# A gated two-layer attention kernel: weighted sums once per head group, fp32 transposes of rounded rows, and VectorE's other work at other steps

## The reference

```python
x = x + tanh(g_xattn[0]) * L0_xattn(layernorm(x), ctx)      # 16 heads of 16; keys: 120 of ctx, then 256 of x
x = x + tanh(g_ffn[0])   * L0_ffn(layernorm(x))             # input rounded by one scale for all of x; ternary weights
x = x + tanh(g_xattn[1]) * L1_xattn(layernorm(x), ctx, lens)# rmsnorm, 256x256 product, plus a decaying recurrence over ctx
x = x + tanh(g_ffn[1])   * L1_ffn(layernorm(x))             # each row rounded by its own scale, int8 product
# L0_ffn:  q = clip(round(x / i_scale), -128, 127);  q @ q_weight.T * w_scale * i_scale + bias
# L1_ffn:  q = clip(round(row / row_scale), -127, 127);  (q @ q_rhs) * row_scale * rhs_scale
```

## Time and profile before

| | us |
|---|---|
| median of 3 runs (lowest, highest) | 1207.3 (1205.55, 1210.32) |
| time of the profiled execution | 1205.75 |
| its span, first to last instruction | 1204.0 |
| TensorE busy | 1098.1 |
| VectorE busy | 930.2 |
| ScalarE busy | 869.0 |
| GpSimd busy | 698.9 |

### The profile page before, as it was taken

How to read it: one execution, slowest core, us unless ns; L and a number is a source line. 1 busy time by engine, 2 the same in 40 slices (tenths; PEclk the granted TensorE clock), 3 DMA queues, 4 the chain that set the end, 5 groups by cost and what they waited for, 6 DMA issues and landing times.

```text
span 1204.0 us, 33614 instructions
## 1 busy us (share of the span) xinstructions
PE 1098.1 (91%) x8458; PEld 667.5 (55%) x8458; DVE 930.2 (77%) x2360; ACT 869.0 (72%) x1794; POOL 698.9 (58%) x1259
## 2 busy tenths in 40 slices
PE   3599999999999999999999999999999948878784
PEld 3355555555555555555555555555555426666663
DVE  3877777777777777777777777777777647999997
ACT  2167777777777777777777777777776658999984
POOL 5355555666555555555555666665554136777766
PEclk9599999999999999999999999999999978999997
DMA  4233334343433333333333333333333101222222
GB/s 131 73 93 96 97 99 103 101 101 103 105 102 102 101 102 98 108 101 95 95 95 95 98 102 102 100 103 99 98 91 87 38 21 42 77 84 80 79 86 80
DMA packets 158681, 110.19 MB, mean 92 GB/s; under 512 B 17154, under 2 KB 154788, under 8 KB 158628
## 3 DMA queue, kind: packets, MB, share of 16 engines
q1 hardware_dynamic: 156900, 108.78, 33.3%
q10 hardware_dynamic: 1728, 0.79, 0.2%
HBM read 30.30 MB, written 16.29 MB: 39 GB/s over the span
## 4 chain that ended last, share of the span: by engine, by line
PE 64%; DVE 15%; issue 9%; POOL 3%; DMA 2%; SPq 2%; ACT 2%; DVEq 1%; POOLq 0%; ACTq 0%
PE pv_ps L621 14%; PE ms_ps L606 13%; PE st_ps L596 12%; PE misc L644 9%; PE misc L652 5%; PE misc L647 4%; DVE neg L789 2%; PE aux L668 2%; DVE am L1170 2%; DMA q<-parts 2%; DVE xs L1159 2%; DVE probs L1203 1%; PE aux L673 1%; SPq L398 1%; PE aux L662 1%
## 5 line engine op out<-in xcount | busy, mean ns | idle before, releaser
L789 DVE TENSOR_REDUCE neg<-ms_ps 128x1 f32<-128x376 f32 x1024 | 531.9, 544 | 206.7 <-PE ms_ps L606 200.7
L883 ACT ACTIVATE probs<-st_ps 128x512 f32<-128x512 f32 x768 | 451.3, 599 | 173.7 <-PE st_ps L596 98.3
L606 PE MATMUL ms_ps<-k,q 96*128 96x376 bf16 x1024 | 336.0, 329 | 13.5 <-DVE neg L789 5.4
L596 PE MATMUL st_ps<-q,k 99*128 99x256 bf16 x1536 | 295.5, 274 | 0.1
L621 PE MATMUL pv_ps<-probs,v 128*32 128x256 f32 (+1 forms) x3072 | 245.4, 391 | 0.6 <-ACT oT L899 0.4
L596 PEld LDWEIGHTS st_ps<-q,k 99*128 99x128 bf16 x1536 | 134.5, 98 | 91.8 <-ACT probs L883 28.3
L606 PEld LDWEIGHTS ms_ps<-k,q 96*128 96x128 bf16 x1024 | 98.7, 96 | 144.7 <-DVE neg L789 79.0
L644 PE MATMUL misc<-xnT,wqkvT 128*128 128x256 f32 x512 | 156.8, 391 | 1.5 <-ACT xnT L904 1.5
L511 POOL TENSOR_TENSOR xs<-xs,bias_p 128x256 f32 (+1 forms) x64 | 45.2, 726 | 142.8 <-ACT xn L941 142.8
L621 PEld LDWEIGHTS pv_ps<-probs,v 128*32 128x32 f32 (+1 forms) x3072 | 60.5, 108 | 117.7 <-issue 93.1
L541 POOL TENSOR_TENSOR parts<-qk,parts 128x632 bf16<-128x632 f32 x64 | 88.7, 1386 | 13.2 <-POOL parts L539 13.2
(11 more groups left out here) (187 smaller groups left out, 1775.3 us busy)
## 6 DMA issues: line engine op xcount, KB each, us to landing
k<-parts SPq DMA_DIRECT2D x384, 94.0 KB, 2.8
q<-parts SPq DMA_DIRECT2D x384, 64.0 KB, 2.5
xs<-in_x SPq DMA_DIRECT2D x32, 256.0 KB, 2.8
out_dram<-xn SPq DMA_DIRECT2D x32, 256.0 KB, 2.2
cx<-in_ctx SPq DMA_DIRECT2D x32, 240.0 KB, 3.4
recurrence_input<-u_in SPq DMA_DIRECT2D x32, 120.0 KB, 2.3
plug<-plugs SPq DMA_DIRECT2D x32, 120.0 KB, 3.4
powers<-gath SPq DMA_DIRECT2D x32, 120.0 KB, 3.2
```

The source lines that it names most:

```text
L596: mm = pe.matmul(st_ps[u % SR][:, j * S:(j + 1) * S], k6[0:KM, r, h, k * P:(k + 1) * P], q6[0:KM, r, h, :], start=True, stop=True)
L606: pe.matmul(ms_ps[t][:, 0:KEYS], q6[0:KR, r, h % HU, t * P:(t + 1) * P], k6[0:KR, r, h % HU, 0:KEYS], start=True, stop=True).then_inc(s_ms, 1)
L789: dve.tensor_reduce(neg[:, m, t, h % HU:h % HU + 1], ms_ps[t][:, 0:KEYS], AX.X, ALU.max, negate=True).then_inc(s_red, 1)
L883: act.activation(probs[:, u % PR, :], st_ps[u % SR][:, :], ACT.Exp).then_inc(s_exp, 1)
```

## The change

The ring `probs` grows from 8 to 12 slots. The three weighted sums of a group of heads are issued one behind the other, at steps 1, 7, 13 and 19, in place of one at each odd step; the third of each group stands where it stood. The maxima are counted 1, 1, 2, 1, 2, 1. VectorE's other work moves: the first `bn_stats` from step 2 to 1, the update of xs from 12 to 13, line 836 from 14 to 15, line 842 from 17 to 18, the largest values from 21 to 19, the least values from 23 to 7 of the next iteration (in the last iteration to 21). In the row stage the two casts of ScalarE (1224, 1230) and VectorE's line 1208 go, line 1203 adds ROUND in the place of its clip, TensorE transposes the fp32 rows with ROUND still in them, and the copies out of PSUM (1241, 1247) take ROUND off.

```diff
-    PR = 8
+    PR = 12
-            counts = [1, 2, 1, 2, 1, 1] * NG
+            counts = [1, 1, 2, 1, 2, 1] * NG
                     if u == 1 and live(b - 1):
-                        attend(b - 1, opp, NG * NKT - 1)
-                    elif u % 2 and u > 1 and live(b):
-                        attend(b, par, (u - 3) // 2)
+                        for k in range(NKT):
+                            attend(b - 1, opp, (NG - 1) * NKT + k)
+                    elif u % (2 * NKT) == 1 and u > 1 and live(b):
+                        for k in range(NKT):
+                            attend(b, par, (u // (2 * NKT) - 1) * NKT + k)
...
-                    if u == 2 and live(b + 3):
+                    if u == 1 and live(b + 3):
-                    if u == 12 and live(b - 1):
+                    if u == 13 and live(b - 1):
-                    if u == 14 and live(b - 1):
+                    if u == 15 and live(b - 1):
-                    if u == 17 and live(b - 1):
+                    if u == 18 and live(b - 1):
                         own_wait(dve, s_x1, (b - 1) * 6 + 2)
...
                             dve.bn_aggr(mvt[:, t, :], bn1[:, t, :]).then_inc(s_x1, 1)
-                    if u == 21 and live(b - 1):
+                    if u == 19 and live(b - 1):
                         dve.tensor_reduce(mx1[:, bass.ds((b - 1) * T, T)], xs[:, b - 1, :, :], AX.X, ALU.max).then_inc(s_x1, 1)
-                    if u == 23 and live(b - 1):
+                    if u == 7 and live(b - 2):
+                        dve.tensor_reduce(mn1[:, bass.ds((b - 2) * T, T)], xs[:, b - 2, :, :], AX.X, ALU.min).then_inc(s_x1, 1)
+                    if isinstance(b, int) and b == LAST and u == 21:
                         dve.tensor_reduce(mn1[:, bass.ds((b - 1) * T, T)], xs[:, b - 1, :, :], AX.X, ALU.min).then_inc(s_x1, 1)
...
-        tq_ps = ms_ps[0][:, :].bitcast(BF16)
-        t3_ps = ms_ps[1][:, :].bitcast(BF16)
+        tq_ps, t3_ps = ms_ps
...
-                    pe.wait_ge(r_s, B + 1)
+                    pe.wait_ge(r_q, B + 1)
                     wait(pe, r_cq, B)
-                    transposes(tq_ps, qq[q], identb, r_tq)
+                    transposes(tq_ps, yq[q], ident, r_tq)
...
-                    pe.wait_ge(r_s3, B + 1)
+                    pe.wait_ge(r_q3, (B + 1) * 4)
                     wait(pe, r_c3, B)
-                    transposes(t3_ps, q3[q], identb, r_t3)
+                    transposes(t3_ps, y3[q], ident, r_t3)
...
-                        ins = dve.tensor_scalar(y[:, t, :], y[:, t, :], am3[:, 1, t:t + 1], 127.0, ALU.mult, ALU.min)
+                        ins = dve.tensor_scalar(y[:, t, :], y[:, t, :], am3[:, 1, t:t + 1], ROUND, ALU.mult, ALU.add)
                     ins.then_inc(r_q3, 1)
-                if has_q:
-
-                    dve.wait_ge(r_q3, cq + 4)
-                    dve.tensor_scalar(y, y, ROUND, ROUND - 127.0, ALU.add, ALU.max).then_inc(r_q3, 1)
...
-                    act.activation(qq[q], yq[q], ACT.Relu, bias=cst[:, 0:1]).then_inc(r_s, 1)
...
-                    act.activation(q3[q], y3[q], ACT.Identity, bias=cst[:, 1:2]).then_inc(r_s3, 1)
...
-                    act.activation(qqT, tq_ps[:, 0:KT * S].rearrange("p (k r) -> p k r", k=KT), ACT.Identity,
-                                   bias=cst[:, 2:3]).then_inc(r_cq, 1)
+                    act.activation(qqT, tq_ps[:, :].rearrange("p (k r) -> p k r", k=KT), ACT.Identity,
+                                   bias=cst[:, 1:2]).then_inc(r_cq, 1)
...
-                    act.copy(q3T, t3_ps[:, 0:KT * S].rearrange("p (k r) -> p k r", k=KT)).then_inc(r_c3, 1)
+                    act.activation(q3T, t3_ps[:, :].rearrange("p (k r) -> p k r", k=KT), ACT.Identity,
+                                   bias=cst[:, 1:2]).then_inc(r_c3, 1)
```

More of the change, by code:

```diff
@@ L189, in flamingo_two_layers @@
         bparts = parts[:, :, :, :].rearrange("p m a c -> p (m a c)")
-        qq = [bparts[:, i * T * C:(i + 1) * T * C].rearrange("p (t c) -> p t c", t=T) for i in range(2)]
-        q3 = [bparts[:, i * T * C:(i + 1) * T * C].rearrange("p (t c) -> p t c", t=T) for i in range(2, 4)]
         qqT = bparts[:, 4 * T * C:5 * T * C].rearrange("p (k r) -> p k r", k=KT)
@@ L258, in flamingo_two_layers @@
         r_q = sem("r_q")
-        r_s = sem("r_s")
         r_tq = sem("r_tq")
@@ L269, in flamingo_two_layers @@
         r_q3 = sem("r_q3")
-        r_s3 = sem("r_s3")
         r_t3 = sem("r_t3")
@@ L1167, in body @@
                     Bq, qq_ = n - QUANT, half(i, par, QUANT)[1]
-                    cq, y = Bq * 5, y3[qq_]
+                    cq, y = Bq * 4, y3[qq_]
                     dve.wait_ge(r_y3, (Bq + 1) * T)
@@ L1216, in body @@
                 n = i * 2 + par
[L1218 to L1222, removed]
-                        act.wait_ge(r_tq, B - 1)
-                    act.activation(qq[q], yq[q], ACT.Relu, bias=cst[:, 0:1]).then_inc(r_s, 1)
-                if live(n - MM2):
-                    B, q = n - MM2, half(i, par, MM2)[1]
-                    act.wait_ge(r_q3, (B + 1) * 5)
-                    if live(B - 2):
-                        act.wait_ge(r_t3, B - 1)
-                    act.activation(q3[q], y3[q], ACT.Identity, bias=cst[:, 1:2]).then_inc(r_s3, 1)
                 if live(n - MM1):
@@ L1259, in body @@
                     if live(B - 2):
-                        own_wait(act, r_s3, B - 1)
+                        own_wait(act, r_t3, B - 1)
                     for t in range(T):
@@ L1265, in body @@
                     if live(n - 2):
-                        act.wait_ge(r_s, n - 1)
+                        act.wait_ge(r_tq, n - 1)
                     for t in range(T):
```

## The result

The changed kernel takes 1213.84 us (median of 11 runs, 1210.94 to 1218.27) against 1207.3: a ratio of 1.0055, 95% interval 1.0039 to 1.0071. It is slower by about 6.5 us.

What follows compares the result with a forecast made beforehand. TensorE was taken to bound the attention stage, with a landing slack of only 0.41 us, and VectorE the row stage. 1205.75 + 24 (attention) - 15 (row stage) = 1214.8, plus 1.5 for the median: 1216; range 1190 to 1234.

Steps and rivals of the forecast that it cites:

- The chain: Attention stage: loop from the score of heads 0 through line 842, GpSimd's splits and the landing to that score; 29.24 us.
- Legs (g) and (h): GpSimd to the end of the split maxima, 3.10 us; then splits and SyncE's twelve issues to the landing, 10.84 us.
- Part (b) and (d): Attention stage: the two groups of three joined sums on the loop, 1.53 us each.
- Rival 3: Attention stage: joined sums take 0.57 us each, time 1226; chance 0.13.
- (c): Steps 8 to 12 and the head of 13: 5.14 us, plus 0.54 stall of step 13's sums for ScalarE's exponential.
- (a): From the score of heads 0 at step 6 through `aT` to the entry of the joined sums: 1.09 us.
- (e): Steps 14 to 17 and up to the score of 18: 4.05 us, plus 0.25 stall for VectorE.
- A second sign of the same chain: `neg0`, near step 20, already waits for GpSimd and will wait longer with line 842 a step later; not counted again.
- 29 iterations: Attention stage: about 29 iterations carry the whole loop, 0.83 us longer than 28.41 each: +24 us.
- rival 4: Row stage: two thirds of its gain go back to GpSimd's adds, line 1195 waiting in every iteration; 1226; chance 0.10.
- Rival 1: Attention stage: batch stays at 28.4 us as ScalarE or VectorE catch up, only the row stage counts; 1192; chance 0.20.
- Rival 2: Attention stage: landings come earlier, the loop is no bound, TensorE's saving arrives but for half a microsecond; 1163; chance 0.10.

## Why the prediction was right, and where its steps were not

1216 was forecast, 1213.84 measured, and both stages came out with the sign and nearly the size of their terms (+24 and -15 forecast, +22.5 and -15.3 measured).

- **The chain.** Right, and shown: its score stands 0.14 behind the landing, and shortening its first leg by 0.52 shortened the batch by 0.52. Legs (g) and (h) were 3.10 and 10.93, forecast 3.10 and 10.84.
- **Three joined sums at 0.48.** Right: 1.44 for three. Part (b) and (d) were sized 1.53 because I gave the last half 0.33 as in the earlier trace rows; the measured 1.44 is 6 x 0.24. Two of them lie in the leg, 0.18 too much. Rival 3 (0.57) is out: no pass between the sums showed the weight load.
- **ScalarE's 0.54 in (c).** Wrong, and this is most of the leg's 0.55 of error; the other differences, 0.22 more in (c), 0.11 more in (a) and 0.18 less in the sums, nearly cancel. ScalarE's own time was read rightly. From the end of the sums of step 7 (430.06) to the copy of the negated maxima are 1.23 us, forecast 1.24, and from the copy to the exponential of step 11 are 3.78, forecast 3.79. In time:

```profile
431.29 0.36 ACT L891 COPY negT<-aux 24x256 bf16<-24x256 bf16 x1 [0.65 <-PE aux L658]
431.77 0.75 ACTq L893 DMA_DIRECT2D q<-negT  x1
432.70 1.08 ACT L883 ACTIVATE probs<-st_ps 128x512 f32<-128x512 f32 x2 [1.04 <-PE st_ps L592]
433.67 0.71 ACT L929 COPY cxp<-cx 120x128 f32<-120x128 f32 x2
434.27 0.61 ACT L883 ACTIVATE probs<-st_ps 128x512 f32<-128x512 f32 x1
434.76 0.42 ACT L948 ACTIVATE gath<-gath 120x256 f32<-120x256 f32 x1
435.07 1.09 ACT L883 ACTIVATE probs<-st_ps 128x512 f32<-128x512 f32 x2
```

  The exponential at 434.27 is that of step 10, that of step 11 stands behind `gath` at 435.07, as in the kernel before, whose rows between those of the earlier trace rows are:

```profile
421.95 0.60 ACT L883 ACTIVATE probs<-st_ps 128x512 f32<-128x512 f32 x1
422.44 0.42 ACT L948 ACTIVATE gath<-gath 120x256 f32<-120x256 f32 x1
```

  What failed is who waits for it. The sums of step 13 did not:

```profile
435.42 0.85 PE L617 MATMUL pv_ps<-probs,v 128*32 128x256 f32 x12
```

  They began while the exponential of step 11 was still running (it ended at 435.68). Only the third sum of the three needs it, by the count that `attend` waits for, and that sum comes 0.96 us behind the first, at 436.38, with 0.7 us to spare. The step had the whole group wait for what its last member needs. (The 1.4 us that it gives the issue and the gap behind it hold the copy too; the idle time in the earlier trace rows is 1.05. Nothing rests on it.)
- **VectorE's 0.25 in (e).** Right in size: 0.21 at steps 17 and 18, which lie in the leg, and 0.07 at step 19, behind it.
- **What replaced the 0.54.** Not forecast: 0.31 ahead of `scores_t` of step 0, for the small transfer of the negated maxima, and further stalls of 0.05 to 0.1. In the sum they cost nothing of their own, for the first lies in the part of the turn where TensorE would else wait for the landing.
- **`neg0`.** "A second sign of the same chain, not counted again" held for the time (0.79 of stall, and the batch still 28.94), but as a price it was under-read: with single sums the same late line 842 cost 1.5 us a batch through `neg0`, not through the landing. The move was cheap only beside joined sums.
- **29 iterations.** 31 distances between batches hold 18.8 of the 22.5 us: 3.1 in one batch of 32.09 instead of 28.94, the other 15.7 at 0.5 each. 2.0 us lie in the setup (first batch at 69.74, before 67.7), 1.6 behind the last batch. So the +24 came near by luck, through two errors that nearly cancel: a chain 0.30 too long, 8.7 us in 29 turns, and 6.7 us outside the turns that were left out. That the setup and the one long batch are the change's doing is not shown: the kernel with o3 earlier and line 842 at 18 has one batch of 32.04 as well, but the setup also varied from 66.8 to 70.1 us among kernels with the same one.
- **The row stage.** Right: 206.0 us. In its steady rounds two take 11.82 us where they took 12.57, so a batch gains 0.38, forecast 0.44; 12.2 us of the 15.3 lie between the first and the last batch's update (forecast 14), 2.5 behind the last (forecast 1). Line 1208's place is gone and the lock with GpSimd's adds stayed nearly as it was, every second iteration (but for four slow ones in a row, of which the rows below show one, line 1196 took 0.78 and 0.39 by turns, as the earlier trace rows had 0.85 and 0.39 for line 1195), so rival 4 is out. Line 1204 grew from a mean of 337 ns to 394, 0.11 a batch. In time:

```profile
1060.20 0.84 DVE L1196 TENSOR_SCALAR probs<-probs 128x512 f32<-128x512 f32 x1
1060.97 0.23 DVE L1200 BATCH_NORM_AGGREGATE mv<-bn 128x2 f32<-128x6 f32 x2
1061.12 0.58 DVE L1204 TENSOR_SCALAR probs<-probs,am 128x256 f32<-128x256 f32 x2
1061.62 0.86 DVE L1154 SCALAR_TENSOR_TENSOR probs<-st_ps,ls,w1s 128x256 f32<-128x256 f32 x2
```

  The same row stage took 205.98 to 209.6 us in the kernels that had it; two rounds took 11.8 us in some and 12.2 in others, and which of the two a kernel falls into is not settled.
- **Rival 1** (the chain stays at 28.4, 1192 us) comes true in its batch, 28.42, in the changed kernel with line 842 at 17, though the median there is 1202. What it lacked was that step, not a faster ScalarE. Rival 2 (the saving arrives, a batch some 1.0 shorter) is out with 28.94.

What stays open is the 0.74 us at step 12 with line 842 at 16. The small transfer's last packet came 1.82 us after its issue there and the matmul 1.34 after that, against 1.69 and 0.73 in the changed kernel, and in half of the batches its issue starts within 0.04 us of one of SyncE's, where the changed kernel has 0.3 between them. Those batches are the slower ones, 3.2 to 3.3 from the issue to the matmul, but the others take 2.9 to 3.2, more than the changed kernel's 2.42. But with line 842 at 15 they are 0.3 apart too, and the matmul still came 1.07 behind the last packet. So where that time goes isn't settled; only the row load is excluded.

## What to carry to other kernels

Close the loop on paper: follow one buffer from its reader back through splits, queues and the instruction that lets them start, until the same reader one iteration earlier; once that loop sets the time, no saving off it shortens it, and a small instruction on it that is issued later lengthens it by the whole delay. When instructions are grouped, make only the member that needs a result wait for it, in the program and in the forecast: here the first two sums of the group had nothing to wait for. And when a leg is shortened, look at which instructions now run side by side: here one step of a 0.24 us aggregation moved the time by 27 us, by the trace mostly through a write that has nothing to do with it.

## What the runs showed of the hardware

- VectorE's write of `gath`, two inputs in SBUF, took 0.415 us alone and ended 0.27 to 0.30 us behind the end of GpSimd's subtraction (two inputs, 1.38 us) whenever it began inside it: 1.59 us when 0.07 behind its start, 1.57 at 0.08, 1.40 at 0.28. Inside GpSimd's copy (one input, 0.72 us) it was the same: 0.88 us at 0.11, 0.82 at 0.17, 0.42 at 0.59, where nothing is left to see of it. GpSimd's time did not change.
- 24 column-tiled fp32 matmuls of 32 columns, each with a weight load of its own over all rows, follow at 0.24 us for every four, across sums as within one. The first sum costs 0.1 more behind a full-width matmul.
- From the issue of the 12 KB transfer by ScalarE to its last packet are 1.66 to 1.85 us, and to the matmul that waits for it 2.3 to 3.2 in the means of the kernels, with the same bytes.
